# Softmax division, a value product, padding, taps and dt of a fused layer moved to other places in four in-order instruction streams

## What is computed

```python
# attention, per batch: q from layernorm(x), k and v from the context
qh, kh, vh = split(q @ Wq + bq), split(k @ Wk + bk), split(v @ Wv + bv)
attn = softmax(qh @ kh.T / sqrt(32) + mask * -1e9)
x = x + merge(attn @ vh) @ Wo + bo
# state-space block on xn = layernorm(x)
x_, z = split(xn @ in_proj_w)                        # 1024 channels each
x_ = silu(depthwise_conv(x_, 4 taps) + conv_b)
B, C, d = x_ @ x_proj_w                              # 16 + 16 + 1 columns
dt = softplus(d * dt_w + dt_b)
h[t] = exp(dt[t] * A) * h[t-1] + (dt[t] * x_[t]) * B[t]     # 16 states a channel
y = (sum_n h * C + x_ * D) * silu(z)
x = x + y @ out_proj_w
# feed-forward on layernorm(x): relu(quant_linear(., w1, b1)), quant_linear(., w2, b2)
```

## Time and profile before

| what | value |
| --- | --- |
| median of 3 runs | 2130.1 us (2128.94 to 2133.53) |
| the profiled execution's own time | 2131.11 us |
| its span, first to last instruction | 2129.3 us |
| mean granted PE clock | 0.973 of 2.4 GHz |
| intervals 2 to 14, from L1577 to L1577 | 1485.8 us, 13 of them |
| interval 15 | 109.5 us |
| tail and feed-forward block | 284.2 us |

### The profile page before, as it was taken

The page is one execution under the profiler, slowest core; times in us unless marked ns, Lnnn a source line. Parts: engine busy times, 40 slices in busy tenths (PEclk is TensorE's granted clock), DMA queues, the critical chain, the costliest instruction groups (busy, mean ns, idle before and its releaser), DMA issues.

```text
span 2129.3 us, 37673 instructions
## 1 busy us (share of the span) xinstructions
PE 1922.3 (90%) x11723; PEld 1378.7 (65%) x11738; DVE 1858.4 (87%) x2311; ACT 1679.3 (79%) x4617; POOL 469.1 (22%) x395
## 2 busy tenths in 40 slices
PE   6999899999989899989899999989999999567799
PEld 4677676766667666667676666767666767456444
DVE  1543899999999999999999999999999999989678
ACT  2547879888888888888979888888888898766584
POOL 1000213122313131231312222313122141200013
PEclk9999999999999999999999999999999999788899
DMA  6721333333333233333332333333333332410214
GB/s 206 274 82 66 75 95 71 87 79 70 94 75 99 70 97 70 91 89 85 85 94 68 72 87 75 94 80 98 71 95 72 84 87 76 119 41 11 70 39 138
DMA packets 93163, 187.95 MB, mean 88 GB/s; under 512 B 18736, under 2 KB 39872, under 8 KB 87872
## 3 DMA queue, kind: packets, MB, share of 16 engines
q1 hardware_dynamic: 78448, 133.32, 19.6%
q0 software_dynamic: 14544, 52.96, 13.0%
HBM read 116.12 MB, written 17.18 MB: 63 GB/s over the span
## 4 chain that ended last, share of the span: by engine, by line
PE 41%; ACT 22%; issue 17%; DVE 17%; DMA 1%; DVEq 1%; SPq 0%; ACTq 0%; POOL 0%; POOLq 0%
ACT dA L1323 11%; PE bank L903 9%; PE bank L993 7%; PE bank L894 5%; DVE hb L1633 3%; ACT Pr L1218 3%; PE bank L940 3%; PE bank L974 3%; PE bank L1095 3%; PE bank L1117 3%; DVE hb L1667 2%; DVE hb L1656 2%; PE bank L1058 2%; DVE hb L1661 2%; PE bank L869 2%
## 5 line engine op out<-in xcount | busy, mean ns | idle before, releaser
L1323 ACT ACTIVATE dA<-dt,A_sb 128x124 f32<-128x124 f32 x2048 | 612.0, 390 | 36.2 <-DVE dt L1618 34.7
L1661 DVE TENSOR_TENSOR_SCAN hb<-dA,hb 128x2048 f32<-128x2048 f32 x116 | 513.2, 4424 | 43.1 <-ACT dA L1323 39.2
L894 PE MATMUL bank<-ctxT,wk_sb 128*128 128x256 f32 x2048 | 457.2, 381 | 8.1 <-ACT ctxT L1151 8.1
L903 PE MATMUL bank<-wv_sb,ctxT 128*128 128x512 f32 x1024 | 462.8, 595 | 0.9 <-ACT ctxT L1151 0.9
L894 PEld LDWEIGHTS bank<-ctxT,wk_sb 128*128 128x128 f32 x2048 | 383.6, 190 | 67.9 <-ACT ctxT L1151 11.0
L903 PEld LDWEIGHTS bank<-wv_sb,ctxT 128*128 128x128 f32 x1024 | 186.6, 191 | 194.3 <-issue 193.0
L1417 POOL DMA_DIRECT2D hb<-hb x101 | 91.6, 907 | 904.7 <-DVE hb L1667 893.0
L1667 DVE TENSOR_TENSOR hb<-hb,BC 128x2048 f32<-128x2048 f32 x115 | 273.1, 2375 | 1.5
L1656 DVE TENSOR_TENSOR hb<-u,BC 128x2048 f32<-128x2048 f32 x116 | 265.8, 2291 | 5.6 <-DVE u L1623 2.6
L993 PE MATMUL bank<-xn2T,win_sb 128*128 128x128 f32 x2048 | 243.0, 281 | 0.8 <-ACT xn2T L1243 0.7
L993 PEld LDWEIGHTS bank<-xn2T,win_sb 128*128 128x128 f32 x2048 | 240.9, 198 | 3.1 <-ACT xn2T L1243 1.3
(11 more groups left out here) (156 smaller groups left out, 2629.1 us busy)
## 6 DMA issues: line engine op xcount, KB each, us to landing
hb<-hb POOLq DMA_DIRECT2D x101, 512.0 KB, 4.6
ctx_sb<-in_ctx_dram SPq DMA_DIRECT2D x64, 512.0 KB, 3.6
BC<-bcd_dram SPq DMA_DIRECT2D x32, 1024.0 KB, 6.5
maskb<-in_mask_Bx1x1xS_fk_dram SPq DMA_DIRECT2D x64, 128.5 KB, 3.4
wstage<-in_L_ffn_w_dram SPq DMA_DIRECT2D x4, 2048.0 KB, 11.0
x_sb<-in_x_dram SPq DMA_DIRECT2D x16, 256.0 KB, 3.3
win_sb<-in_L_attn_in_proj_w_dram SPq DMA_DIRECT2D x1, 4096.0 KB, 24.9
bo_sb<-bias_dram SPq DMA_DIRECT2D x64, 64.0 KB, 2.0
```

The costliest lines, as they stand in the source:

```text
L894: last = pe.matmul(bank[6 + j][:, (m % 2) * KF:(m % 2 + 1) * KF], wk_sb[:, c, m * P:(m + 1) * P], ctxT[:, c, :], start=(c == 0), stop=(c = ...
L903: last = pe.matmul(bank[h][:], ctxT[:, c, h * P:(h + 1) * P], wv_sb[:, c, :], start=(c == 0), stop=(c == DC - 1))
L1323: last = act.activation(dA[:, c % 2, n * BT:(n + 1) * BT, 1:], dt[:, c, :].rearrange("p (b s) -> p b s", s=S)[:, :, 1:], ACT.Exp, scale=A_ ...
L1661: ins = dve.tensor_tensor_scan(flat, dA[:, c % 2].rearrange("p n s -> p (n s)"), flat, 0.0, ALU.mult, ALU.add)
```

## The change

It moves work to other places in the order; nothing is computed differently.

- In batch 0 of an interval, place `a` (the first decays and the C product) comes behind `softmax` instead of ahead of it, and `keys_copy(…, 0)` behind `normalise` and `mamba_rows` instead of ahead of them. So the division is issued earlier.
- In batch 0 the first half of the value product runs on PE straight behind the keys, ahead of the norm's transposes. Its copy (`values_copy`, now a name of its own) stays where it was.
- `kv_transpose` waits for V's two halves one by one: the transposes into bank 0 no longer wait for the copy out of bank 1.
- `mamba_pad` and `mamba_taps` go by halves: pad 0, taps 0 to 3, pad 1, taps 4 to 7.
- `mamba_dt` is split: dt is formed at place `t` of batch 2, ahead of the last chunk's sum; u = dt x_ is formed where it was (`mamba_u`). Chain steps 29 and 30 go to `t`, 31 to `p`.
- The first decays of a tile go in four pieces of 8 to `b`, `p`, `c`, `w` instead of two of 16 to `p` and `w`.

```diff
-                  (2, "a"): range(28, 29), (2, "b"): range(29, 32)}
+                  (2, "a"): range(28, 29), (2, "t"): range(29, 31), (2, "p"): range(31, 32)}
-        BEGIN_DECAYS = {(2, "p"): ((0, 0), (0, 1)), (2, "w"): ((1, 0), (1, 1)), (3, "m"): ((2, 0),), (3, "n"): ((2, 1),),
+        BEGIN_DECAYS = {(2, "b"): ((0, 0),), (2, "p"): ((0, 1),), (2, "c"): ((1, 0),), (2, "w"): ((1, 1),),
...
-                    place("a")
+                    if b > 0:
+                        place("a")
                     if here:
                         part.softmax(g)
+                    if b == 0:
+                        place("a")
                     place("m")
...
                     if following:
                         part.kv_keys(g + 1, b, ta, tm, to, more)
+                    if following and b == 0:
+                        part.kv_values(g + 1, 0)
+                    if following and b > 0:
                         part.keys_copy(g + 1, 0)
                     if here:
                         part.normalise(g)
                     if b == 0 and front:
                         part.mamba_rows(tm)
+                    if following and b == 0:
+                        part.keys_copy(g + 1, 0)
                     place("n")
...
                     if b == 2 and front:
                         part.mamba_softplus(tm)
                         part.mamba_gate(tm, keys)
+                        part.mamba_dt(tm)
                     place("b")
...
                     if b == 0 and front:
-                        part.mamba_taps(tm)
+                        part.mamba_taps(tm, 0)
+                        part.mamba_pad(tm, 1)
+                        part.mamba_taps(tm, 1)
...
+                    if following and b > 0:
+                        part.kv_values(g + 1, 0)
                     if following:
-                        part.kv_values(g + 1, 0)
+                        part.values_copy(g + 1, 0)
...
                     if b == 2 and front:
-                        part.mamba_dt(tm)
+                        part.mamba_u(tm)
...
-                    wait(pe, v_copied, 2 * g)
-                    wait(pe, xnT_copied, 1 if isinstance(g, int) and g == 1 else rows)
                     pe.wait_ge(ctx_loaded, 16 * (g + 1))
                     for i in range(2):
+                        if i == 0:
+                            wait(pe, v_copied, 2 * g - 1 if not isinstance(g, int) or g else 0)
+                            wait(pe, xnT_copied, 1 if isinstance(g, int) and g == 1 else rows)
+                        else:
+                            wait(pe, v_copied, 2 * g)
...
+                def mamba_u(self, t):
+                    if isinstance(t, int) and t == LAST:
+                        dve.wait_ge(tail_kept, 2)
+                        dve.wait_ge(tail_fed, item(PREV, IC - 1))
+                    else:
+                        wait(dve, y_ready, t)
                     for i, half in enumerate((slice(0, IC // 2), slice(IC // 2, IC))):
                         dve.wait_ge(dt_step, 10 * t + 9 + i)
```

More of the change, by code:

```diff
@@ L355, in tail @@
             part.weigh(PREV, 4)
-            part.mamba_pad(LAST)
-            part.mamba_taps(LAST)
+            part.mamba_pad(LAST, 0)
+            part.mamba_taps(LAST, 0)
+            part.mamba_pad(LAST, 1)
+            part.mamba_taps(LAST, 1)
             part.feed(PREV, 5)
@@ L378, in tail @@
             part.mamba_dt(LAST)
+            part.mamba_u(LAST)
             part.decays(LAST, ((0, 0), (0, 1)))
@@ L422, in schedule @@
             part.kv_values(0, 0)
+            part.values_copy(0, 0)
             part.kv_values(0, 1)
+            part.values_copy(0, 1)
             part.kv_keys(0, None, None, None, None, False)
@@ L505, in interval @@
                     if b == 0 and front:
-                        part.mamba_pad(tm)
+                        part.mamba_pad(tm, 0)
                     if b == 2 and front:
@@ L545, in interval @@
                         part.kv_values(g + 1, 1)
+                        part.values_copy(g + 1, 1)
                     if b == 2 and here and more:
@@ L580, in kv_values, with values_copy @@
             def kv_values(self, g, h): pass
+            def values_copy(self, g, h): pass
             def load_x(self, t): pass
@@ L601, in mamba_in, with mamba_pad, mamba_taps @@
             def mamba_in(self, t, keys): pass
-            def mamba_pad(self, t): pass
-            def mamba_taps(self, t): pass
+            def mamba_pad(self, t, q): pass
+            def mamba_taps(self, t, q): pass
             def mamba_conv(self, t): pass
@@ L614, in mamba_dt, with mamba_u @@
             def mamba_dt(self, t): pass
+            def mamba_u(self, t): pass
             def mamba_skip(self, t): pass
@@ L1160, in keys_copy, with values_copy @@
                                        ACT.Identity, bias=bqkv[:, 1, m:m + 1]).then_inc(k_copied, 1)
-                def kv_values(self, g, h):
+                def values_copy(self, g, h):
                     wait(act, o_psum, g)
@@ L1243, in mamba_transpose, with mamba_pad, mamba_taps @@
                     act.copy(xn2T[:].rearrange("p c q -> p (c q)"), bank[6][:]).then_inc(xn2T_copied, 1)
-                def mamba_pad(self, t):
-                    wait(act, dt_step, 10 * t)
-                    for q in range(2):
-                        act.wait_ge(in_psum, 4 * t + q + 1)
-                        act.copy(xpad[:, 16 * q:16 * (q + 1), TAPS - 1:],
-                                 bank[6 + q][:].rearrange("p (e s) -> p e s", s=S)).then_inc(xpad_ready, 1)
-                def mamba_taps(self, t):
-                    if isinstance(t, int) and t == 0:
-                        act.wait_ge(w_quantised, 8)
-                    wait(act, u_ready, 2 * t)
-                    wait(act, bcd_psum, t)
-                    act.wait_ge(xpad_ready, 2 * t + 2)
-                    for c in range(IC):
+                def mamba_pad(self, t, q):
+                    if q == 0:
+                        wait(act, dt_step, 10 * t)
+                    act.wait_ge(in_psum, 4 * t + q + 1)
+                    act.copy(xpad[:, 16 * q:16 * (q + 1), TAPS - 1:],
+                             bank[6 + q][:].rearrange("p (e s) -> p e s", s=S)).then_inc(xpad_ready, 1)
+                def mamba_taps(self, t, q):
+                    if q == 0:
+                        if isinstance(t, int) and t == 0:
+                            act.wait_ge(w_quantised, 8)
+                        wait(act, u_ready, 2 * t)
+                        wait(act, bcd_psum, t)
+                    act.wait_ge(xpad_ready, 2 * t + q + 1)
+                    for c in range(4 * q, 4 * q + 4):
                         act.activation(xs[:, c, :].rearrange("p (b s) -> p b s", s=S),
@@ L1418, in scans, with mamba_pad @@
                                            ).then_inc(hb_added[c % 2], 16)
-                def mamba_pad(self, t):
+                def mamba_pad(self, t, q):
+                    if q == 1:
+                        return
                     wait(pool, dt_step, 10 * t)
```

2 lines of the change are left out of this document (1 added, 1 removed).

## The result

The changed kernel takes 2108.3 us (median of 5 runs, 2105.6 to 2109.0) beside 2130.7 us (2128.9 to 2133.5) for the kernel before: 0.989 of the time, with a 95% interval of 0.9877 to 0.9903. That is 22.3 us gained of the 37 forecast. The time lies inside the range of 2085 to 2112, near its upper end, where I had put the case that the wait in batch 3 stays.

The account below looks back on a forecast made before the run. DVE and PE, both nearly full, hold each other up in turn. Thirteen intervals of 111.2 us save 40.2, +0.3 for interval 15, less 2.6 for thin margins: −37.3, so 2093 us; range 2085 to 2112.

Parts of the forecast that it names:

- the case that the wait in batch 3 stays: Rival: most of DVE's 1.59 us wait for decays in batch 3 stays; interval 112.8, total 2111 us; chance 0.17.
- 113.71 − 0.26 − 0.63 − 1.59 = 111.2 us: Interval length after the change: 0.26 off after batch 0, 0.63 in batch 2, 1.59 in batch 3.
- the reciprocal's wait: DVE, batch 0: the reciprocal now stands ahead of the C product and waits about 1.1 us for ACT.
- the C product: DVE, batch 0: starting after POOL's addition is over, it takes 2.29 us instead of 3.23.
- The wait for scores in batch 1: DVE, batch 1: its 0.49 us wait for PE's scores goes, 1.6 in the long interval.
- its own signs: Wrong if batch 3's decays' wait exceeds 1 us, the C product still takes 3.2 us, or interval lengths still alternate.
- the wait of 1.59 goes as a whole or nearly so: DVE, batch 3: decays end by about 1259.9 instead of 1262.27, so the 1.59 us wait goes; margin nil.
- PE keeps a lead of 0.8 us over DVE, and idles for the rest: PE, batch 1: its transposes wait for the division, which can start at 1199.4 instead of 1200.25.
- PE's clock no longer reaches DVE: All intervals: both alternating kinds, 113.71 and 115.14 us, become one of 111.2 us.
- the clock stays the bound: Rival: PE's clock still falls, an input product costs 1.0 us more; interval 112.5, total 2117 us; chance 0.06.
- The slower case: Rival, batch 2: first decays wait for DVE's dt, PE stands still some 1.5 us each interval; 2146 us; chance 0.06.
- The collision with POOL: Rival, batch 0: DVE's C product still overlaps POOL's addition, +0.94 us each interval; 2105 us; chance 0.10.

Follow-up runs that it names:

- the bridge: The changed kernel with seven extra 128x128 products, results unused, on PE in batch 1 where it waits for the division: 2095.4 us, ratio 0.9833.
- the same work put behind the transposes: The changed kernel with seven extra products, results unused, on PE behind the transposes of the probabilities in batch 1: 2116.3 us, ratio 0.9925.
- the kernel before, bridged in batch 0: The kernel before with thirteen extra products, results unused, on PE in batch 0 ahead of the norm's transposes: 2130.7 us, ratio 0.9998.
- the two bridged versions: The changed kernel with seven extra PE products in batch 1: 2095.4 us; the same with place a also back ahead of softmax in batch 0: 2089.1 us.

## Why the prediction was right, and where it was off

*Right* are most terms of the sum, and the length of an interval that nothing disturbs. "113.71 − 0.26 − 0.63 − 1.59 = 111.2 us" is met within 0.4: 111.57 us in the two undisturbed intervals, 111.60 with the bridge in nearly all, and then 2095.4 us against the 2093 forecast. Term by term: the reciprocal's wait, about 1.1 forecast, is 1.11; the C product, 2.29 forecast, is 2.29. The sums start 7.40 us after the interval's start instead of 7.12, so the net of the two is +0.28 against +0.23. The wait for scores in batch 1 (0.49) and that of batch 2 (0.63) are gone. PE's waits of 3.2 and 1.9 us are 0.83 and 0.49. The Trainium skill's rule on the shared port (SBUF — State Buffer, "SBUF: two separate sides") is nearly borne out where they do overlap: 0.70 us lost for 0.85 of overlap.

*By its own signs it was wrong.* It called itself wrong "if the decays' wait in batch 3 is still over 1 us", and that wait is 1.18. It also expected a clock of 1.00 (0.98 in eleven intervals) and no wait of PE above 1.5 us (1.63). The time lies in the range only because the range reached up to the case that the wait in batch 3 stays; the middle of the forecast is 15 us too low.

*The term that was mis-sized* is batch 3: "the wait of 1.59 goes as a whole or nearly so". It went by 0.4 and stayed, at 1.10 to 1.19, in 11 of 13 intervals. The thirteen intervals take 1463.1 us, and 13 times the undisturbed 111.56 would be 1450.3: the slow clock and this wait are 12.9 of the 15 us missing. The undisturbed interval is 0.36 us longer than the sum, 4.7 in all, of which I had set 2.6 aside; the head's 1.1 stands against interval 15 and the tail, which are 0.9 shorter than forecast. The text's own numbers did not carry the term either: "1.4 to 2.1 us ahead" of 1262.27 is 1260.9 to 1260.2, not "about 1259.9", so against a DVE at 1259.9 they left 0.3 to 1.0 us of wait. I had given this case 0.17, with 2111 us, and it is the one that came.

*The step that failed* stands ahead of it: "PE keeps a lead of 0.8 us over DVE, and idles for the rest", and with it "PE's clock no longer reaches DVE". I had seen that the division in batch 1 waits for the reciprocal behind DVE's scan, and that PE would idle there. What I did not carry on is what follows an idle PE in this kernel, though the earlier trace rows showed it in batch 0. The transposes and the value product behind the new wait of 1.63 us run in part at 1.2 GHz and take 1.5 us more, which is more than the lead. The weighing product of batch 2 ends 72.2 us after the interval's start instead of 71.7 before; I had it 0.8 sooner. V's copy waits for it, xnT follows 0.8 us sooner instead of 2, and the decays of batch 3 come that much late. That PE's being late does this is shown by the bridge (1.5 us given back, the wait gone) and by the same work put behind the transposes (clock 1.00, wait back).

My rival "the clock stays the bound" had the mechanism and the wrong place: I priced it at the input product, behind pieces of 1 to 1.4 us, and not at the longest of the new waits. It was no rival to the batch 3 case but what brought it about. Its sum was wrong as well: 1485.8 − 13 × 112.5 is 23.3 us gained, so 2107 us and not 2117. The thirteen intervals took 112.55 on average, and with the right sum this case, which had 0.06, would have stood nearest to the 2108.3 measured.

*Right for the time, but not worth making.* I put the division and the halves at about nothing, and each undone gives 2106.7 and 2105.2. The slower case (PE standing for DVE's dt) did not come: dt alone gains 13 us. The collision with POOL did not come either; POOL's addition was over 0.35 us ahead of the product, a thin margin.

## What to carry to other kernels

When an edit gives an engine slack, look for the place where it will now stand still, and read from the trace what that engine did after its last such wait: here PE lost 1.5 us behind a wait of 1.6, and so the slack turned into a delay. Between two engines that are each about 90% busy, an instruction moved ahead in a third engine's queue can merely choose who waits, as the decays of batch 3 did here; the parts that gained took work into a wait already there. A part that is worth nothing should be tried again when the bound has moved: the C product's old place gained nothing beside the late PE and 6 to 9 us without it.

## What the runs showed of the hardware

The granted clock fell behind waits of PE of 1.3 us (division part undone), 1.63 (the changed kernel, 0.79 over the following 8 us), 1.76 (value product of batch 1 ahead), 1.87 (the kernel before, bridged in batch 0) and 2.27 us (halves undone), in stretches where PE was otherwise nearly always busy. The Trainium skill (TensorE: Matmul & The Clock Gate, "What's actually happening") has activity open the gate and idling close it, which agrees in direction.

The length of one wait does not decide. The same 1.62 us wait at 849 was followed by full clock. So were, in six intervals of the kernel with dt's part undone, waits of 1.6 and 2.5 us, and in ten intervals with the extra products behind it the wait of 1.6 us.

What had not been expected is that the fall moves. Bridged in batch 0 of the kernel before, it came behind the wait for xnT. Relieved in batch 1 of the changed kernel, it came behind the next wait of that batch. In the two bridged versions, where the longest wait of PE left in an interval is 1.1 and 0.9 us from interval 4 on, it stayed away in every interval from 2 to 14. What decides between one interval and the next of the same kernel, no run here tells.
